# Mean squares of projected heads: the scale inside ScalarE's squaring, epsilon as a 129th column of the sum

## The reference

```python
def rms_norm(x, scale):
    var = jnp.mean(jnp.square(x), axis=-1, keepdims=True)
    return x * jax.lax.rsqrt(var + EPS) * scale          # EPS = 1e-6, last axis: H = 128
...
q = jnp.einsum('btd,ndh->btnh', x, q_kernel)             # 16 heads of 128, on layernorm(x)
kv = jnp.einsum('bsd,ckdh->cbskh', x, kv_kernel)         # 8 heads of 128
k, v = (kv[0], kv[1])
q = rms_norm(q, q_norm_scale)
k = rms_norm(k, k_norm_scale)
q, k = apply_rope(q, positions), apply_rope(k, positions)
mask = (j <= i) & (i - j < WINDOW)
probs = jax.nn.softmax(where(mask, qg * ATTN_SCALE @ k, min), axis=-1)
enc = probs @ v
x = x + einsum(enc, out_kernel)
```

## Time and profile before

| | us |
|---|---|
| median of 3 runs | 732.27 |
| runs | 732.14, 732.27, 892.83 |
| profiled execution, device time | 732.23 |
| its span, first to last instruction | 730.4 |
| PE busy | 704.2 (96% of the span) |
| DVE busy | 496.1 (68%) |
| ACT busy | 403.7 (55%) |
| POOL busy | 359.0 (49%) |

### The profile page before, as it was taken

The page is one execution under the profiler, slowest core; times in us unless marked ns, Lnnn a source line. Parts: engine busy times, 40 slices in busy tenths (PEclk is TensorE's granted clock), DMA queues, the critical chain, the costliest instruction groups (busy, mean ns, idle before and its releaser), DMA issues.

```text
span 730.4 us, 14854 instructions
## 1 busy us (share of the span) xinstructions
PE 704.2 (96%) x4296; PEld 628.6 (86%) x4296; DVE 496.1 (68%) x1698; ACT 403.7 (55%) x1205; POOL 359.0 (49%) x508
## 2 busy tenths in 40 slices
PE   4799999999999998999999999999999999999998
PEld 3589999999999987888879999999999999878887
DVE  6998888888888898768757454444445444567443
ACT  4576666666676663523246555555555555554221
POOL 3898888888887884002179342323232325317000
PEclk9999999999999999999999999999999999999999
DMA  6010110101020021100011010101101100000000
GB/s 230 1 44 2 44 45 1 43 0 43 0 101 29 0 87 73 44 1 1 15 59 59 1 59 3 57 14 45 33 25 51 49 0 14 0 15 1 1 30 29
DMA packets 9002, 24.64 MB, mean 34 GB/s; under 512 B 896, under 2 KB 3072, under 8 KB 8832
## 3 DMA queue, kind: packets, MB, share of 16 engines
q1 hardware_dynamic: 8240, 22.55, 8.9%
q10 hardware_dynamic: 720, 1.57, 0.6%
HBM read 23.07 MB, written 1.05 MB: 33 GB/s over the span
## 4 chain that ended last, share of the span: by engine, by line
PE 90%; DVE 6%; issue 1%; POOL 1%; DMA 1%; ACT 1%; DVEq 0%; POOLq 0%; ACTq 0%
PE bank L620 12%; PE bank L309 12%; PE bank L328 11%; PE bank L303 11%; PE bank L360 8%; PE bank L281 7%; PE bank L340 6%; PE bank L349 5%; PE bank L362 4%; PE bank L280 4%; PE bank L371 3%; PE bank L663 2%; PE bank L659 2%; PE bank L687 1%; DVE probs L445 1%
## 5 line engine op out<-in xcount | busy, mean ns | idle before, releaser
L433 ACT ACTIVATE probs<-scores,negmax 128x128 f32<-128x128 f32 (+1 forms) x256 | 115.6, 452 | 43.1 <-DVE negmax L481 42.4
L462 DVE TENSOR_TENSOR enc_lo<-bank,enc_hi 128x256 fp32r<-128x256 f32 x128 | 54.2, 423 | 116.8 <-PE bank L281 110.5
L384 ACT COPY probs_t<-bank 128x384 f32<-128x384 f32 x128 | 61.1, 477 | 120.2 <-PE bank L349 120.2
L525 POOL TENSOR_TENSOR a_hi<-raw_a,zero 128x384 fp32r<-128x384 f32 (+2 forms) x69 | 53.0, 769 | 111.7 <-PE bank L340 108.3
L445 DVE TENSOR_SCALAR probs<-probs,rinv 128x128 f32<-128x128 f32 (+1 forms) x256 | 88.0, 386 | 4.5
L360 PE MATMUL bank<-probs_t,v 128*128 128x256 f32 x256 | 77.1, 383 | 5.1 <-DVE enc_lo L462 4.7
L281 PE MATMUL bank<-qk 128*128 128x256 f32 x256 | 76.5, 381 | 0.0
L538 POOL TENSOR_TENSOR rms_r<-meansq,neg_half 128x3 f32<-128x3 f32 x64 | 58.2, 909 | 34.8 <-DVE meansq L515 34.6
L328 PE MATMUL bank<-b_hi,enc_hi 128*128 128x256 f32 x256 | 74.9, 292 | 0.0
L328 PE MATMUL bank<-b_hi,enc_lo 128*128 128x256 f32 x256 | 72.3, 283 | 0.0
L328 PE MATMUL bank<-b_lo,enc_hi 128*128 128x256 f32 x256 | 72.3, 282 | 0.0
(11 more groups left out here) (124 smaller groups left out, 2032.6 us busy)
## 6 DMA issues: line engine op xcount, KB each, us to landing
raw_a<-in_wa SPq DMA_DIRECT2D x10, 768.0 KB, 4.4
raw_a<-in_wa SPq DMA_DIRECT2D x9, 512.0 KB, 4.0
raw_b<-in_wb SPq DMA_DIRECT2D x16, 256.0 KB, 2.6
x<-in_x SPq DMA_DIRECT2D x4, 256.0 KB, 6.5
w_a<-in_w2t SPq DMA_DIRECT2D x1, 1024.0 KB, 4.9
raw_a<-in_wax SPq DMA_DIRECT2D x2, 512.0 KB, 3.8
raw_b<-in_wdown SPq DMA_DIRECT2D x2, 512.0 KB, 3.8
raw_a<-in_wa ACTq DMA_DIRECT2D x1, 512.0 KB, 5.1
```

The lines of the kernel that those rows point to most:

```text
L433: nc.scalar.activation(probs[:, c % 4, c0:c1], scores[:, c % 2, c0:c1], ACT.Exp, bias=negmax[:, c % 2, r:r + 1], scale=-1.0, accum_out=row ...
```

## The change

ScalarE's square takes a scale of 128 to the power -1/2 on its input, so that the squares come out already divided by 128, and writes them with a gap: three groups of 128 columns at a pitch of 129. GpSimd fills the three gap columns once, at the start, with 1e-6. VectorE's sum runs over 129 columns and so gives the mean square plus epsilon itself, straight into `meansq`. The instruction that divided and added is gone, with its buffer and its semaphore. The wait for `rp` (the power of the item two before has been taken, so that its `meansq` is free) moves from that instruction to the sum, and ScalarE's next square waits for `ms` where it waited for `ss`. Both are signalled by the same sum.

```diff
-        sumsq = sb("sumsq", [P, 2, 3])
         meansq = sb("meansq", [P, 2, 3])
...
-        squares = gate[:, 0, 0:384]
+        squares = gate[:, 0, 0:3 * (DH + 1)].rearrange("p (a d) -> p a d", a=3)
...
                 if L == 0:
 
-                    need(act, s["ss"], it, m)
-                    nc.scalar.activation(squares, bank[PJ_BANK + m % 2][:, 0:384], ACT.Square).then_inc(s["sq"], 1)
+                    if it is None and m == 0:
+                        act.wait_ge(s_eps, 1)
+                    need(act, s["ms"], it, m)
+                    nc.scalar.activation(squares[:, :, 0:DH], bank[PJ_BANK + m % 2][:, 0:384].rearrange("p (a d) -> p a d", a=3),
+                                         ACT.Square, scale=float(DH) ** -0.5).then_inc(s["sq"], 1)
...
                     need(dve, s["sq"], it, m + 1)
-                    nc.vector.reduce_sum(sumsq[:, m % 2, :], squares.rearrange("p (a d) -> p a d", a=3),
-                                         AX_X).then_inc(s["ss"], 1)
+                    need(dve, s["rp"], it, m - 1)
+                    nc.vector.reduce_sum(meansq[:, m % 2, :], squares, AX_X).then_inc(s["ms"], 1)
                     need(dve, s["vev"], it, m + 1)
                     need(dve, s["tq"], it, m - 1)
                     nc.vector.tensor_tensor(rot_a[:, m % 2, :], ps[:, 0:384],
                                             cos_t[:, t % 2, :, :].rearrange("p a d -> p (a d)"), ALU.mult)
-                    need(dve, s["ss"], it, m + 1)
-                    need(dve, s["rp"], it, m - 1)
-                    nc.vector.tensor_scalar(meansq[:, m % 2, :], sumsq[:, m % 2, :], 1.0 / DH, RMS_EPS,
-                                            ALU.mult, ALU.add).then_inc(s["ms"], 1)
                     need(dve, s["radd"], it, m - 1)
...
+            nc.gpsimd.memset(squares[:, :, DH:DH + 1], RMS_EPS).then_inc(s_eps, 1)
```

More of the change, by code:

```diff
@@ L152, in build @@
         s_scl, s_w2 = sem("scales_loaded"), sem("w2_loaded")
-        s_zero, s_half, s_scq = (sem(n) for n in ("zero_set", "half_set", "qscale_made"))
+        s_zero, s_half, s_eps, s_scq = (sem(n) for n in ("zero_set", "half_set", "epsilon_set", "qscale_made"))
         s_sin, s_cos, s_second = (sem(n) for n in ("sin_made", "cos_made", "second_head_tables"))
@@ L156, in build @@
         names = ("scores", "max", "exp", "rinv", "pnorm", "pt", "ptev", "pv", "ehi", "elo", "op", "opadd",
-                 "proj", "vproj", "qkev", "vev", "sq", "ss", "ms", "rp", "rot", "radd", "roped", "tq", "tqev",
+                 "proj", "vproj", "qkev", "vev", "sq", "ms", "rp", "rot", "radd", "roped", "tq", "tqev",
                  "a0hi", "a0", "ahi", "a", "bhi", "b")
```

## The result

The changed kernel takes 737.68 us (median of 6 runs, 736.97 to 738.19) beside 732.85 for the kernel before on the same chip. The ratio is 1.0071, 95% interval [1.0061, 1.0081]: 0.7% slower, well under the 2% that a measurement of this kernel can tell from nothing by itself, but outside its interval. The profiled execution took 737.95 with a span of 736.2, so 5.7 and 5.8 us more than the profiled execution of before. By the ratio the loss is 5.2 us, and the two medians lie 4.8 us apart. One execution of before, at 892.83 us, does not enter the ratio.

A forecast was written before the change was run, and what follows sets the result against it. TensorE was taken to bound the kernel, 96% busy, with VectorE's room 0.60 us a slot. Early slots +1.3 and the loop +6.4 gave +7.7 us on 732.27, so 740.0 us; range 731.2 to 743.5.

The forecast's parts named there:

- The meeting of addition and probs: Steady slot, from the sum's start R: GpSimd's addition at R+1.57 blocks VectorE's probs at R+1.60; next sum at R+4.18.
- the 0.08 from rot_b's end to the addition: Steady slot: GpSimd's addition, released by rot_b, starts 0.08 us after rot_b ends; called the step most likely to fail.
- 53 x 0.12 = 6.4: Loop from the eleventh item on: 53 slots, VectorE 0.12 us slower than TensorE's pace in each, 6.4 us in all.
- the upper bound: Loop: if GpSimd's addition takes 1.07 us, the slot is 4.25 and the loop's loss 10 us.
- The early 1.3: Early slots: -0.3 earlier power, -0.4 old meeting moved, +0.7 one newly stalled slot, +1.3 next three slots; sum +1.3 us.
- The 1.3 in the three slots after: Three early slots with GpSimd behind with splits and VectorE near TensorE's pace: 0.4 to 0.5 us lost each, 1.3 together.
- The -0.3 for the earlier power: Near 18.15 us: GpSimd's power no longer waits for the removed instruction but for the sum, saving 0.3 us.
- TensorE waits for rot_b from then on: After the early slots: TensorE's 1.1 us between rot_b and its projection is used up; it waits 0.12 us a slot.
- Rival 1: Loop: no collision that counts, or only every second slot; not slower, 731.3 to 732.5 us; chance 0.22.
- Rival 2: Loop: first probs gets in and delays the addition, second probs waits for it; slot 4.50, 757 us; chance 0.05.
- Rival 3: Loop: stall comes, but VectorE regains 0.05 to 0.12 us a slot counted as serial; 732.5 to 737 us; chance 0.10.
- The small costs: Sum over 387 columns for 384: under 0.01 us a slot; square in three pieces: nothing to 0.02, taken as nothing.

The follow-up runs named there:

- e1: Changed kernel, with GpSimd's power also waiting for rot_b, so that its addition comes after both probs; 732.0 us, ratio 1.000.
- e2: Kernel before, with its divide-and-add instruction kept but moved directly behind the sum, ahead of rot_a; 754.15 us, ratio 1.0301.
- e3: Changed kernel's scaled square and 129-column sum, but a small VectorE instruction (times 1, plus 0) kept at the old place; 732.35 us, ratio 1.0004.
- e5: Changed kernel, with only VectorE's reciprocal moved ahead of rot_b, so the first probs starts before the addition; 732.6 us, ratio 1.0002.
- e6: Changed kernel, with GpSimd's addition of 384 columns cut into two of 192; 734.17 us, ratio 1.0021.
- e7: Like e1, with the probs of the last slots of both attentions moved from VectorE to ScalarE; 731.12 us, ratio 0.9988.
- e4: Changed kernel, with VectorE's reciprocal and both probs moved ahead of rot_b of the same slot; 732.89 us, ratio 1.0012.
- e8: Changed kernel, with GpSimd's power also waiting for rot_b, but only from item 12 on; 733.17 us, ratio 1.0016.
- e9: Changed kernel, with GpSimd's power also waiting for rot_b, but only in the first twelve items; 736.64 us, ratio 1.0067.

## Why the prediction came out as it did

The forecast was 740.0 us, range 731.2 to 743.5, with 0.92 on a difference under 2%. It came out at 737.68 beside 732.85; in the loop the mechanism is the forecast's, and the size is smaller; in the first slots it was another.

- **The meeting of addition and probs: right, to 0.02 us.** R+1.57 and R+1.60 were forecast, R+1.55 and R+1.58 stand in the trace; x at R+2.83 as forecast; the next sum at R+4.17 for R+4.18. The step called most likely to fail, the 0.08 from rot_b's end to the addition, holds (rot_b ends at 254.15, the addition starts at 254.22). e1 and e2 show that this is the cause, from both sides, and e3 that the arithmetic is not.
- **53 x 0.12 = 6.4: mis-sized, 5.2.** The excess over TensorE's pace is 0.101 a slot (4.164 against 4.063), and 51 slots have it. The addition's 1.07 of the earlier trace rows, the upper bound, did not come: it takes 1.00 or 1.01. The 1.07 was an addition held by the probs ahead of it, as shown under e5, and once the addition is the first of the two nothing holds it.
- **The early 1.3: mis-sized, and wrong inside.** It measured 0.84 in the profiled pair and 0.9 by the table, so near 1.3 by luck. Two of its terms came as written: the slot of item 5 is 0.46 shorter (3.958 to 3.504) and that of item 6 is 0.72 longer (2.792 to 3.513). The 1.3 in the three slots after did not. GpSimd is behind there, as the prediction itself said, and so its additions start at R+1.85 to R+2.65, behind the start of both probs (in item 7 the second probs holds the addition, 1.16 for 1.00); item 7 even gains 0.48. In its place stand two things that I had not looked for: VectorE's xn and a_lo, blocked by the earlier additions between 18 and 31 us, and the stretch at 1.2 GHz, whose price is open. The -0.3 for the earlier power is not to be seen: what GpSimd gained there, xn lost.
- **"TensorE waits for rot_b from then on": wrong.** It waits for x, which is 1.9 us later in VectorE's slot and frees the single output bank, and L327 is the matmul that is late. The prediction took the 1.1 us between rot_b and the projection for TensorE's room; it never mattered. The loss per slot is the same, since in a closed loop the slower engine sets the pace whichever wait passes it on.
- **Rivals.** Rival 1 (no collision) asked for 0.1 us more on GpSimd, and e1, with more than that, gives its 731.3 to 732.5: 732.0. (The 731.3 is 0.3 lower than the rival's own terms make it, 732.27 - 0.7 = 731.6.) Rival 2 asked for the addition to be held by a probs that came first; in e5 a probs does come first, and the addition starts regardless and takes its 1.00. The rival charged the whole rest of the first probs, where an overlap of 0.12 costs nothing, and 0.26 from the end of the addition to x, which is 0.07 when it is the second probs that was held. That the two engines can hold each other either way was right. Rival 3 (a milder stall) ended at 737, just below what was measured; its mechanism, VectorE picking up 0.05 or more of steps counted as serial, is worth 0.02 at most (0.101 for 0.12).
- **The small costs: right.** e3 finds the square and the sum within 3 ns of the old ones.

The Trainium skill's rule ("SBUF — State Buffer", section "Who interferes with whom") says that the first to issue gets the shared ports for its whole instruction. For the addition and probs the runs agree with the length (1048 to 1116 ns, until the addition is over) and with both directions (an addition of 1.16 behind a probs 0.06 ahead of it), though a probs 0.02 ahead still lost. And a_lo, an instruction with both inputs in SBUF, waits as the page states (1.12 for 0.41). They differ for the power, which runs beside probs in e1 with probs at 286 ns. The reverse is in the traces: in the kernel before 24 powers take 0.98 to 1.00 us, as the first of the earlier trace rows does, and each of these ends 0.04 us behind the second probs, while the other 34 that met a probs take 0.86.

What stays open: why the power does not hold up probs, and how the early 1.40 divides. e6 has the late transposes without a fall of the clock and loses 0.83 by the table's first column (19.24 to 27.94), which would leave some 0.6 for the stretch at 1.2 GHz; but its addition is cut too, and no kernel changes the clock alone. The executions of one kernel do not agree on that price either. In e5 the six with a mean granted clock of 0.997 or 0.998 average 732.5 us and the four at 1.000 732.7; in e1 the four at 0.998 average 732.1 and the six at 1.000 732.2; in e7 it is 732.7 for three at 0.998 and 730.8 for six at 1.000.

## What to carry to other kernels

Removing an instruction from an engine with idle time gained nothing here (e1 has the whole change without the collision, at 1.000), but it hands its result to the next engine earlier, and the question is what that engine then runs beside: here GpSimd's 1.0 us addition moved by 0.45 us onto VectorE's probs. Price such a collision by what exceeds the slot's room, not by its length (0.8 us blocked cost 0.10 a slot here and nothing in e5), and mend it with a wait or an order that moves the phase, as e1 did with one wait. Before trusting a difference in the first tens of us of two single profiles, anchor it at an instruction behind the point where TensorE's matmuls have become short.

## What the runs showed of the hardware that was not expected

- VectorE and GpSimd hold each other, by the time of the start. An addition 0.03 ahead of probs holds it for 1.05 us, and so did one that was 0.02 behind the earlier trace rows. A probs 0.06 ahead gets through in its 0.35, and the addition takes 1.16. An overlap of up to 0.13 us costs the addition nothing (e5: 1.00).
- The lock is by instruction: with two additions of 192 columns a waiting probs gets in between them (640 ns), and the next is caught by the second (703 ns).
- When the first of two probs was held, the second starts right at the end of the addition and VectorE's next instruction 0.27 us behind that end, in the loop as in the earlier trace rows. When the second was held (e5), the next starts 0.07 behind the end.
- The granted clock fell to 0.50 for 3.4 us in every profiled execution in which TensorE had waited 1.87 us or more for xT_lo just before (1.87 in the changed kernel, e4, e5 and e8, 2.06 in e2), and in none where that wait was 1.53 or less (1.53 in e6, 1.37 before, 1.35 in e3, 0.70 in e1, e7 and e9). It is not the kernel alone that decides: four of e1's ten executions, without a trace, have a mean of 0.998, as one such stretch gives, and four of e5's ten have 1.000.
